# Router ranks taken in PSUM, its exponential from a tanh, and expert groups of two, two and three tiles, in a windowed-attention block with a mixture of experts

## What is computed

```python
x = x + attention(layer_norm(x))          # roll, windows of 49, bias, mask, softmax, projection
t = x.reshape(B, H * W, C)
scores = layer_norm(t) @ gate_w + gate_b
probs = softmax(scores)                   # 4 experts
mask = one_hot(top_k(probs, 2)).sum()     # the lower index wins a tie
masked = probs * mask
masked = masked / (masked.sum() + 1e-9)
h = gelu(einsum(layer_norm(t), w1) + b1)  # every expert, 384 hidden channels
y = einsum(h, w2) + b2
t = t + (masked * y).sum over experts
```

## Time and profile before

| | |
|---|---|
| median of 3 runs | 7973.55 us (7973.3 to 7974.85) |
| profiled execution | 7975.47 us, span 7973.6 us |
| TensorE busy | 83%, granted clock 0.942 on average |
| VectorE, GpSimd, ScalarE busy | 78%, 64%, 59% |
| DMA | 32 GB/s, the queue of the program's transfers 10.3% of its engines |

### The profile page before, as it was taken

How to read it: one execution, slowest core, us unless ns; L and a number is a source line. 1 busy time by engine, 2 the same in 40 slices (tenths; PEclk the granted TensorE clock), 3 DMA queues, 4 the chain that set the end, 5 groups by cost and what they waited for, 6 DMA issues and landing times.

```text
span 7973.6 us, 261448 instructions
## 1 busy us (share of the span) xinstructions
PE 6600.4 (83%) x98944; PEld 5272.3 (66%) x98944; DVE 6203.9 (78%) x15654; ACT 4679.9 (59%) x8959; POOL 5109.5 (64%) x3337
## 2 busy tenths in 40 slices
PE   5888888888888888888888888888888888888887
PEld 4666666666666666666666666666666666666665
DVE  6777777777777777777777778777777777777776
ACT  3566556655565556556565556555655665566554
POOL 3666666666666666666666666666666666666665
PEclk8999999999999999999999999999999999999998
DMA  1111111111111111111111111111111111111110
GB/s 48 32 30 33 31 32 30 33 31 32 29 33 31 32 29 33 32 32 29 32 32 32 30 32 32 32 30 32 32 32 30 32 32 31 32 32 32 32 29 17
DMA packets 168081, 251.65 MB, mean 32 GB/s; under 512 B 44498, under 2 KB 129106, under 8 KB 166738
## 3 DMA queue, kind: packets, MB, share of 16 engines
q1 hardware_dynamic: 166866, 234.90, 10.3%
HBM read 80.58 MB, written 38.54 MB: 15 GB/s over the span
## 4 chain that ended last, share of the span: by engine, by line
PE 38%; DVE 24%; issue 16%; POOL 16%; ACT 6%; SPq 1%; POOLq 0%; DVEq 0%; ACTq 0%; DMA 0%
POOL gexp L435 11%; PE ps_t L1027 7%; PE ps_o L1044 5%; PE ps_s L1007 5%; DVE s_max L739 4%; PE ps_s L1017 3%; PE ps_f L1111 3%; PE ps_f L1113 3%; PE ps_f L1115 3%; DVE geq L848 3%; POOL xr L457 3%; DVE ggt L851 3%; DVE geq L849 3%; DVE gden L860 2%; DVE gsel L853 2%
## 5 line engine op out<-in xcount | busy, mean ns | idle before, releaser
L447 POOL TENSOR_TENSOR g_lo<-g_sb,g_hi 128x784 f16<-128x784 f32 x1536 | 2782.2, 1837 | 998.6 <-ACT g_hi L537 998.1
L546 ACT ACTIVATE g_sb<-ps_f 128x392 f32<-128x392 f32 x3072 | 1526.8, 497 | 221.5 <-PE ps_f L957 220.2
L562 ACT ACTIVATE pt_sb<-ps_t 113x588 f32<-113x588 f32 x1024 | 674.7, 659 | 1529.5 <-PE ps_t L1027 1529.4
L457 POOL TENSOR_TENSOR xr<-y_gated,xr 112x384 f32<-112x384 f32 (+1 forms) x1024 | 905.8, 895 | 985.5 <-DVE y_gated L884 985.5
L1111 PE MATMUL ps_f<-w_hi,g_hi 128*128 128x96 f16 x9216 | 1368.9, 215 | 0.0
L1113 PE MATMUL ps_f<-w_lo,g_hi 128*128 128x96 f16 x9216 | 1367.1, 215 | 0.0
L1115 PE MATMUL ps_f<-w_hi,g_lo 128*128 128x96 f16 x9216 | 1365.0, 215 | 0.0
L557 ACT ACTIVATE p_sb<-s_sub 113x588 f32<-113x588 f32 x1024 | 714.4, 698 | 886.2 <-DVE s_sub L743 886.2
L739 DVE TENSOR_REDUCE s_max<-ps_s 113x12 f32<-113x588 f32 x1024 | 788.8, 770 | 474.5 <-PE ps_s L1017 458.3
L955 PE MATMUL ps_f<-x_hi,w_hi 128*128 128x392 f16 x3072 | 1012.6, 330 | 117.5 <-DVE x_lo L816 111.8
L1007 PE MATMUL ps_s<-bias,sel 128*64 128x392 f16 (+3 forms) x4096 | 536.5, 325 | 686.9 <-DVE s_sub L743 672.7
(11 more groups left out here) (131 smaller groups left out, 14570.4 us busy)
## 6 DMA issues: line engine op xcount, KB each, us to landing
k_st<-qk_hi SPq DMA_DIRECT2D x768, 49.0 KB, 1.9
q_st<-qk_hi SPq DMA_DIRECT2D x768, 49.0 KB, 1.9
xr<-x SPq DMA_DIRECT2D x224, 139.1 KB
out<-xr SPq DMA_DIRECT2D x224, 139.1 KB
xa<-x SPq DMA_DIRECT2D x224, 136.5 KB
k_st<-qk_lo SPq DMA_DIRECT2D x384, 49.0 KB, 2.0
q_st<-qk_lo SPq DMA_DIRECT2D x384, 49.0 KB, 1.9
xa<-x SPq DMA_DIRECT2D x224, 10.5 KB
```

The lines of the kernel that those rows point to most:

```text
L447: nc.gpsimd.tensor_tensor(g_lo[:, slot, 0:TOK], g_sb[:, chunk, :], g_hi[:, slot, 0:TOK], ALU.subtract).then_inc(lo_done, 1)
L457: nc.gpsimd.tensor_tensor(slot, y_gated[:, g % 2, 0:n * C], slot, ALU.add).then_inc(comb_done, 1)
L546: nc.scalar.activation(g_sb[:, chunk, half * STRIP:(half + 1) * STRIP], h_bank[k % 3][:, 0:STRIP], ACT.Gelu, scale=1.0 / WSCALE).then_inc( ...
```

## The change

- The router's compares no longer use the exponentials. `router_a` takes the maximum, subtracts, copies the raw scores to SBUF and compares each expert's score with the others straight from the accumulator bank: `>=` against experts of lower index, `>` against those of higher, which breaks ties without a table. The sum of these is the rank.
- The exponential: ScalarE takes t = tanh of half the scaled score behind its third GELU, and VectorE makes 2 / (1 - t) - 1, which is exp. `gate_exp` is gone from GpSimd. `router_b` keeps three small intermediates in bank 0.
- VectorE's step begins with `router_b`, then chunks 0 to 2, the key spreading, and chunks 3 to 5.
- The experts' groups have 2, 2 and 3 tiles, twelve to a unit, with new places (`GROUPS_AT`, `COMBINES_AT`, `ROUND_AT`, `Y_BANK`), four of them late; `y_gated` has four slots of three tiles.
- In `residual` the combines stand in other places; on GpSimd the late adds wait for `norm2_done`; on TensorE hidden part 1 waits for the tenth late combine; ScalarE no longer waits for `lo_done` before the first GELU.

```diff
-GROUP_TILES = ((0, 4), (4, 3))
-GROUPS_AT = ((0, 1), (2,), (3,), (), (), (4,), (), ())
-COMBINES_AT = ((0,), (1,), (2,), (3,), (), (), (4,), ())
-LATE_GROUPS = (5, 6, 7)
+GROUP_TILES = ((0, 2), (2, 2), (4, 3))
+PARTS = len(GROUP_TILES)
+GROUPS_AT = ((0, 1, 2), (3,), (4,), (5,), (), (6,), (7,), ())
+COMBINES_AT = ((0, 1), (2,), (3,), (4,), (5,), (), (6,), (7,))
+LATE_GROUPS = (8, 9, 10, 11)
-ROUND_AT = ((), (6, 7), (8,), (), (), (9,), (10, 11), ())
+ROUND_AT = ((), (6,), (7,), (8,), (), (9,), (10,), (11,))
-Y_BANK = (5, 7, 6, 5, 7, 7, 4, 7)
+Y_BANK = (5, 7, 6, 5, 7, 6, 7, 7, 7, 4, 7, 4)
...
@@ GpSimd, step
...
                 if a is not None:
                     rsqrt2(a)
-                add(f, u, 5)
-                add(f, u, 6)
-                add(f, u, 7)
-                if a is not None:
-                    gate_exp(a)
+
+                    pool.wait_ge(norm2_done, at(a, 2, 2))
+                for g in LATE_GROUPS:
+                    add(f, u, g)
...
@@ ScalarE
             def gelus(f, k0):
-                if k0 == 0 and not first(f):
-                    act.wait_ge(lo_done, at(f, N_LO))
...
+            def router_tanh(f):
+
+                act.wait_ge(router, at(f, N_ROUTER, 2))
+                nc.scalar.activation(gtanh[:, :, :], gsub[:, :, :], ACT.Tanh, scale=0.5 / WSCALE
+                                     ).then_inc(tanh_done, 1)
...
                 for i in range(8):
                     gelus(f, 3 * i)
+                    if i == 0:
+                        router_tanh(f)
@@ VectorE, residual
                 if before is not None:
-                    combine(before, 5)
+                    combine(before, 8)
                 sums_of(*second_part)
+                if before is not None:
+                    combine(before, 9)
                 centre(*first_part)
                 variances(*second_part)
                 scale(*first_part)
                 centre(*second_part)
                 scale(*second_part)
+                x2_low(f, 0)
                 if before is not None:
-                    combine(before, 6)
-                    combine(before, 7)
-                x2_low(f, 0)
+                    combine(before, 10)
+                    combine(before, 11)
                 x2_low(f, 1)
@@ VectorE, router_a
-                dve.wait_ge(router, at(f, N_ROUTER, 2))
-                V.tensor_scalar(gsub[:, :, :], gsub[:, :, :], 1.0 / WSCALE, None, ALU.mult).then_inc(router, 1)
+                V.tensor_copy(gsc[:, :, :], sc).then_inc(router, 1)
+                dve.wait_ge(router, at(f, N_ROUTER, 3))
+
+                for e in range(EXPERTS):
+                    for f0, f1, beats in ((0, e, ALU.is_ge), (e + 1, EXPERTS, ALU.is_gt)):
+                        if f0 < f1:
+                            ins = V.tensor_tensor(ahead[:, :, e, f0:f1], sc[:, :, f0:f1],
+                                                  gsc[:, :, e:e + 1].broadcast_to([LANES, W, f1 - f0]), beats)
+                ins.then_inc(router, 1)
+                dve.wait_ge(router, at(f, N_ROUTER, 4))
+                V.tensor_reduce(rank[:, :, :], ahead[:, :, :, :], AX.X, ALU.add).then_inc(router, 1)
@@ VectorE, router_b
+                dve.wait_ge(tanh_done, at(f, 1, 1))
+                link(V.tensor_scalar(gden28[:, :, :], gtanh[:, :, :], -1.0, 1.0, ALU.mult, ALU.add))
+                link(V.reciprocal(gden28[:, :, :], gden28[:, :, :]))
+                link(V.tensor_scalar(powers, gden28[:, :, :], 2.0, -1.0, ALU.mult, ALU.add))
+                V.tensor_reduce(gtot[:, :], powers, AX.X, ALU.add).then_inc(router, 1)
                 k[0] += 1
...
@@ VectorE, step
+                router_b(f)
+                for chunk in range(CPE):
+                    round_chunk(f, chunk)
                 if a is not None:
                     spread_keys(a)
-                for chunk in range(2 * CPE):
+                for chunk in range(CPE, 2 * CPE):
                     round_chunk(f, chunk)
-                router_b(f)
@@ TensorE
                     if n == 0 and groups:
                         experts(f, groups.pop(0))
+                        experts(f, groups.pop(0))
...
-                hidden(a, (0, 1))
+                hidden(a, (0,))
+                if f is not None:
+
+                    pe.wait_ge(gated, at(f, N_Y, 11))
+                hidden(a, (1,))
                 gate_scores(a)
```

More of the change, by code:

```diff
@@ L222, in build @@
         gsub = sb("gsub", [LANES, W, EXPERTS])
[L223 to L226, removed]
+        gsc = sb("gsc", [LANES, W, EXPERTS])
+        gtanh = sb("gtanh", [LANES, W, EXPERTS])
+        gden28 = sb("gden28", [LANES, W, EXPERTS])
+        ahead = sb("ahead", [LANES, W, EXPERTS, EXPERTS])
+        rank = sb("rank", [LANES, W, EXPERTS])
         gsel = sb("gsel", [LANES, W, EXPERTS])
@@ L463, in prologue @@
                 rsqrt2((0, 0))
-                gate_exp((0, 0))
             def step(f, a, b, u):
-                first_half, second_half = range(0, CPE), range(CPE, 2 * CPE)
-                for chunk in first_half:
+                for chunk in range(2 * CPE):
                     low_part(f, chunk)
[L470 to L473, removed]
+                for g in range(3):
+                    add(f, u, g)
                 if b is not None:
@@ L477, in step @@
                     low_part(f, chunk)
[L478 to L482, removed]
+                    add(f, u, chunk - CPE)
+                low_part(f, 9)
+                low_part(f, 10)
+                add(f, u, 6)
+                low_part(f, 11)
+                add(f, u, 7)
                 if a is not None:
                     rsqrt2(a)
-                add(f, u, 5)
-                add(f, u, 6)
-                add(f, u, 7)
-                if a is not None:
-                    gate_exp(a)
+                    pool.wait_ge(norm2_done, at(a, 2, 2))
+                for g in LATE_GROUPS:
+                    add(f, u, g)
             schedule(pool, step, prologue)
@@ L683, in setup @@
                     fill(V.memset(lo[ONES_ROW:128, :], 0.0))
+                fill(V.memset(ahead[:, :, :, :], 0.0))
                 V.memset(s_sub[:, :, :, :], 0.0).then_inc(s_ready, 1)
@@ L845, in router_b @@
-                dve.wait_ge(gexp_done, at(f, 1, 1))
-                V.tensor_tensor(gt4, other, mine, ALU.is_gt).then_inc(router, 1)
-                k[0] += 1
-                link(V.tensor_tensor(eq4, other, mine, ALU.is_equal))
-                link(V.tensor_tensor(eq4, eq4, tie.unsqueeze(1).broadcast_to([LANES, W, EXPERTS, EXPERTS]),
-                                     ALU.mult))
-                link(V.tensor_tensor(ggt[:, :, :], ggt[:, :, :], geq[:, :, :], ALU.add))
-                link(V.tensor_reduce(rank[:, :], ggt[:, :, :], AX.X, ALU.add))
@@ L855, in router_b @@
+                link(V.reciprocal(gden28[:, :, :], gden28[:, :, :]))
+                link(V.tensor_scalar(powers, gden28[:, :, :], 2.0, -1.0, ALU.mult, ALU.add))
+                V.tensor_reduce(gtot[:, :], powers, AX.X, ALU.add).then_inc(router, 1)
+                k[0] += 1
+                link(V.scalar_tensor_tensor(out=gsel[:, :, :], in0=rank[:, :, :], scalar=1.5, in1=powers,
                                             op0=ALU.is_lt, op1=ALU.mult))
[L856 removed]
@@ L857, in router_b @@
-                k[0] += 1
-                link(V.tensor_reduce(gden[:, :], gsel[:, :, :], AX.X, ALU.add))
-                link(V.scalar_tensor_tensor(out=gden[:, :], in0=gtot[:, :], scalar=1e-9, in1=gden[:, :],
+                link(V.tensor_reduce(sums, gsel[:, :, :], AX.X, ALU.add))
+                link(V.scalar_tensor_tensor(out=gden[:, :], in0=gtot[:, :], scalar=1e-9, in1=sums,
                                             op0=ALU.mult, op1=ALU.add))
-                link(V.reciprocal(gden[:, :], gden[:, :]))
+                V.reciprocal(inverse, gden[:, :]).then_inc(inverse_done, 1)
@@ L904, in attention @@
                 for n in range(8):
-                    if f is not None and 0 < n < 7:
+                    if f is not None and n:
                         for g in COMBINES_AT[n]:
@@ L910, in attention @@
                     if f is not None and n == 0:
-                        combine(f, 0)
+                        for g in COMBINES_AT[0]:
+                            combine(f, g)
                     if n:
@@ L1103, in experts @@
                 y = y_bank(g)[:, 0:n * C]
-                T.matmul(y, ones16[:, :], b2_16[:, e * 4 * C:e * 4 * C + n * C], start=True, stop=False,
+                T.matmul(y, ones16[:, :], b2_16[:, e * 3 * C:e * 3 * C + n * C], start=True, stop=False,
                          skip_group_check=True)
```

60 lines of the change are left out of this document (22 added, 38 removed).

## The result

The changed kernel takes 7045.48 us (7039.39 to 7048.0 in four runs) beside 7973.99 for the kernel before: ratio 0.883 (95%: 0.882 to 0.885), 929 us faster. Forecast were 7490, range 7240 to 7720: the sign was right, the gain nearly twice the forecast 484, and the time lies outside the range. The profiled execution took 7046.41 us with a span of 7044.6. From one router maximum to the next it is 54.20 us in the mean of 127 units, 61.48 before; forecast 57.64.

What follows compares the result with a forecast made beforehand. VectorE's queue, with its long router, was taken as TensorE's last wait. Gains 4.3 + 1.6 + 0.85 less 0.15 make 6.6 us a unit, less 2.8 for the clock 3.8; over 127 units 483, forecast 7490, range 7240 to 7720.

Steps and rivals of the forecast that it cites:

- What bounds the kernel: No engine is full; TensorE's 5.28 us wait per unit ends with VectorE's queue, where the router takes 10.2 us.
- Step 1, the router: Router first on VectorE: second part of nine small operations takes 2.0 us, ends at 3.6; 8 us off the queue.
- The tanh rival: ScalarE's tanh brings two table loads of 1.28 us, low parts come 0.9 later: 7605; chance 0.10.
- Step 2, the order on SBUF: VectorE's casts and keys run until 10.5, GpSimd's three low parts then until 15.5; second scores at 17.5, not 19.67.
- the forecast's own signs of being wrong: It fails if a cast or key operation takes 2 us, the clock never falls, or a load stands beside the tanh.
- Rival "GpSimd between the casts": Five of VectorE's six casts or keys wait for low parts; VectorE ends at 18.9, gain 1.35 a unit: 7800; chance 0.11.
- Step 3 and the clock: Third scores at 20.3 for 24.6, 4.3 us gained at full clock; TensorE's clock falling costs 2.8 us a unit.
- the sum at the full clock: All gains per unit if the clock never falls: 6.6 us, a unit of 54.8.
- Rival "the clock holds": TensorE's 3.9 us gap leaves the clock up, so each unit gains all 6.6 us: 7132; chance 0.12.
- Step 4, the groups: Expert groups of 2, 2, 3 tiles fit under the softmax pairs' chain on TensorE: 1.6 us a unit gained.
- Step 5, the end: At the unit's end the second scaling is kept clear of GpSimd; the router maximum comes 0.85 us earlier.
- 8 us off VectorE's queue: The router's end on VectorE, ahead of the softmax, comes about 8 us sooner; low parts take back most.

Runs made afterwards that it cites:

- e_hold_low: The changed kernel, but GpSimd's first low part waits until VectorE has cast all six chunks: 7322.25 us, 0.918.
- e_hold_warm: The changed kernel with GpSimd held for six casts, plus seventeen unread matmuls on TensorE before the first groups: 7195.47 us, 0.902.
- e_warm: The changed kernel with ten unread matmuls on TensorE ahead of the first scores: 6970.95 us, 0.874.
- e_old_order: The changed kernel with VectorE's old order (keys, six casts, then the router's second part); first scores wait for the gate: 6777.93 us, 0.850.
- e_router_only: The kernel before with the new router alone, old VectorE order and groups of four and three; late combines as in the changed kernel: 7056.39 us, 0.884.
- e_router_mid: The changed kernel with VectorE's order keys, router's second part, six casts; first scores wait for the gate: 7263.8 us, 0.910.
- e_hold3: The changed kernel, but GpSimd's first low part waits for the third cast instead of the first: 7025.07 us, 0.881.
- e_keys_first: The changed kernel with VectorE's order router's second part, twelve key operations, six casts: 7283.28 us, 0.913.
- e_split: The changed kernel with VectorE's order keys, casts 0 to 2, router's second part, first softmax pair, casts 3 to 5: 6780.56 us, 0.850.

## Why the prediction was right and wrong

The forecast's unit was 61.44 - 3.8 = 57.64; it is 54.20.

- *What bounds the kernel*: right. The router in VectorE's queue was the last wait of the earlier trace rows; the new router alone takes 919 us off, in VectorE's old order.
- *Step 1, the router*: right. The second part takes 1.9 us (L848 to the gate) where 2.0 were forecast, ending at 3.27 for 3.6. The tanh rival is false: the tanh takes 0.22 us and no load stands beside it. The Trainium skill's list of table sets (ScalarE: Activation LUTs, "Table sets: the hidden batching unit") does not put tanh beside gelu; the switch that one would expect by it did not come here: the trace has the one load of 1.28 us before the exponentials.
- *Step 2, the order on SBUF*: this failed. "I expect GpSimd to come in at 10.5" came from one pattern, a low part kept off by casts. Here GpSimd came in behind the second cast; a cast of 2.04 us was one of the forecast's own signs of being wrong. The other pattern was on view: in the earlier trace rows the casts have no keys ahead of them, as the first three have none in the changed order, and there they contended. And "had they gone in turns, the sum is the same" counted all six casts as work that the first groups need. They need the low parts 0 to 2 and the keys only; casts 3 to 5 lie behind both, ahead of the softmax pair. In turns, the needed work is 1.45 + 4.0 + 4.9 = 10.4 us from 3.3, which is 13.7; the keys, the last of it, were done at 13.2. The idle time was 2.38 us, not 3.9. e_hold_low, with GpSimd where I had put it, measures this step: 277 us of the miss of 445.
- *Rival "GpSimd between the casts"* had its mechanism partly right and its time, 7800, wrong on both counts: it took five of six casts as contending, where one cast and two keys do, for the three low parts go in beside the keys; and it did not see that TensorE asks for keys and low parts before it asks for the softmax pair. (Its own terms, 3.6 + 6.9 + 8.2, put VectorE's end at 18.7, not 18.9.)
- *Step 3 and the clock*: its size was off. 2.8 us was taken as if each unit lay 6.9 us low. e_hold_low and e_hold_warm give 56.70 - 54.22 = 2.5 us for that, and only 1.5 for the short stretch of 3.4 us, which half of the units had. With the first units of the images counted in, the full clock is worth an estimated 54.22 + 0.73 / 4 = 54.40 in the mean, so the clock cost 56.36 - 54.40 = 2.0 where 2.8 stood, and the sum at the full clock was 54.84 for these 54.40. Together that is 1.3 us a unit, the 168 us from 7490 to 7322. In the changed kernel 110 of 127 units have the short stretch and 17 none, and by e_warm the fall is worth 0.6 us a unit.
- *Rival "the clock holds"*, 7132, is nearer to the time than the forecast and yet false: the clock fell in 110 of 127 units.
- *Step 4, the groups*: right. From third scores to projection the shown unit needs 24.4 us where it needed 26.0, 1.6 less as forecast; pairs take 3.04 to 3.3, and the 1.6 us are TensorE's two waits of 0.8 for the normalised output, as the forecast's chain had it. Taken back, they cost 171 us, 1.35 a unit. That they are worth 278 in the old order was not foreseen; there the full clock goes with them (low 0.13 in e_old_order against 1.56 in e_router_only).
- *Step 5, the end*: right, 0.96 for 0.85, and the scaling at 0.46.

To the third scores the gain is 24.6 - 19.8 = 4.8 us where 4.3 less 2.8 for the clock was forecast; that is where 3.3 of the missing 3.4 us a unit lie. What the forecast never asked is whether moving the router early was needed once it was short. It took "8 us off VectorE's queue" as due to cost and place together. They were due to the cost, and the new order took 268 us back. The range failed with it: its low end was built from the clock alone and held no case in which the SBUF work ran in another order *and* helped.

## What to carry to other kernels

Of two queues that contend for a memory, list what the waiting engine needs first and sum only that; a total of both queues gives the wrong moment. Small work in PSUM, like this router, is a cover: put it beside the GpSimd work that contends with casts and key operations, and not ahead of it (6778 against 7283 us here). Before moving work that has just become short, price the cheapening alone.

## What the runs showed of the hardware

A low part of GpSimd (1.64 us on its own) that is asked for while VectorE runs casts or keys back to back has two fates, each the same in 127 of 127 units. Asked for during the second cast of a run (the changed kernel, e_router_mid) or during the key behind three casts (e_hold3) it got in at the end of the running operation; from then on the two took turns, a cast stamped 2.04 us and a key 1.83 (free, a run has one every 0.48 and 0.33). Asked for during the cast that follows twelve keys and a cast (e_old_order, e_keys_first, the first part of e_split) it was kept off to the end of the run: the first two have a stamp of 3.86 and 3.84, of which 2.2 is waiting. The low part 3 of the changed kernel, asked for behind ten free keys and a cast, was kept off too (stamp 2.4). The Trainium skill (SBUF — State Buffer, "Who interferes with whom") tells of an exclusive lock held for one instruction; the turns agree, but it does not say who gets the lock next, and a wait through four further casts is more than one instruction's. The old exponential on GpSimd was held up too: stamped 4.79 us in the last unit, where no keys are spread, it has 6.8 to 7.7 in the other 127 and ends 0.06 us behind VectorE's sixth cast in each; at what moment of its stamp it asked for SBUF isn't shown. e_router_mid against e_keys_first shows that nine small operations between keys and casts change the fate. Whether what counts is the number of operations in the run, its length or something else, no run here tells; if it is the number, it lies between four and eleven.

The clock was worth less than its share of the time suggests. In the forecast's order 3.4 us at half speed cost 1.5 and 6.8 cost 2.5. In the changed kernel 3.4 us cost 0.7, and e_warm's new waits for the subtraction and the exponentials took back 0.6 more. That some of the stretch also passes while TensorE idles would explain the rest; it was not measured apart.
